# Work placed in the drain of the last attention layer of a fused conv/attention/MoE network

## The chip, the cores and the metric

The kernel runs on one core of a Trainium2 chip. The metric is the time of one execution on the device, in microseconds; lower is better. Three runs of the kernel before took 864.22, 866.94 and 872.31 us (median 866.94 us).

## The reference

The network has four layers on 16 images of 96 channels and 16 x 16 pixels (4096 tokens of 96 channels). Layers 0 and 1 are convolution-like token mixers, layer 2 is causal attention and a binarised feed-forward net, and layer 3 is causal attention and a mixture of four experts. What bears on this case is layer 3:

```python
t = t + _L3_attn_ref(_ln_t(t), ...)            # causal attention, 6 heads of 16, 256 tokens an image
t = t + _L3_ffn_ref(_ln_t(t), ...)             # the mixture of experts:
scores = jnp.einsum('bsd,de->bse', x, gate_w) + gate_b
probs = jax.nn.softmax(scores, axis=-1)
topk_vals, topk_idx = jax.lax.top_k(probs, 2)
mask = jnp.sum(jax.nn.one_hot(topk_idx, 4), axis=-2)
masked = probs * mask
masked = masked / (jnp.sum(masked, axis=-1, keepdims=True) + 1e-09)
h = jax.nn.gelu(jnp.einsum('bsd,edh->ebsh', x, w1) + b1[:, None, None, :], approximate=False)
y = jnp.einsum('ebsh,ehd->ebsd', h, w2) + b2[:, None, None, :]
out = jnp.einsum('bse,ebsd->bsd', masked, y)
```

## The kernel before, in words

Five engines run programs of their own and meet at semaphores. TensorE (PE) multiplies, VectorE (DVE) and ScalarE (ACT) empty PSUM, GpSimd (POOL) works on SBUF alone, SyncE (SP) issues the DMAs. The order on each engine is written out by hand; nothing is planned at run time. The tokens' residual stream is kept in `tok` (tokens on the partitions), the normed input of the next stage in `xn` (channels on the partitions, 4096 tokens wide), and the residual by channels in `xc`. PSUM is one tile `ps` of eight banks.

**Attention of layer 3.** A loop runs over the 16 images with three units of two heads each: scores (L890, and the mask at L894), maxima (DVE L1414), exponentials (ACT L549), transposes of the probabilities (PE L1071), copies of those to SBUF (ACT L536, DVE L1530), products with the values (PE L959). Scores and queries run two images ahead, so the loop also makes scores and stacked keys for two images that do not exist; SP stacks queries and keys by DMA into `qk` (L251), eight DMAs an image. The work behind an image's attention follows one image later: its outputs to SBUF (ACT L575), transposed (PE L930), normalised (DVE L1440, L1447), transposed back (PE L937), copied (ACT L580), projected (PE L951), added to `tok` (DVE L1454). Statistics of the finished tokens (DVE L1467, L1473), the inverse deviation (ACT L587, L589), the norm (POOL L344 to L349), a transpose (PE L944, `image_back`) and a copy (DVE L1459) put the image into `xn`.

**The drain.** After the loop nothing is left to overlap with. The outputs of image 15 go through the chain just named, and the norms of images 14 and 15 through theirs, one step after the other.

**The start of the mixture.** In the kernel before it follows the drain: PE transposes all of `tok` into channels in eight groups of four 128 x 96 tiles (L1197) and ACT copies each group into `xc` (L737). ACT splits the first two groups of 512 tokens of `xn` into a high part (`split_high`, L741), DVE makes the low part (L1671). PE makes the gate's logits, one 128-token tile of `xn` as weights and a moving operand of four columns, 32 tiles (L1202); a float32 product of this kind is two passes, so there are 64 records. DVE and ACT (L1676 to L1705) turn the logits into gate values; PE transposes these (L1238), DVE copies them to `gate_t` (L1729), and SP stores them and loads them back broadcast over the channels (L277, L274). PE has meanwhile made three steps of the experts' first product (`hidden`, L1217, three float32r matmuls each: high by high, high by low, low by high). From the fourth on it alternates `hidden(n)` and `expert_out(n - 3)` (L1228) for 96 steps in all. Each step's result passes two Gelus on ACT (L754, L757) and a subtraction on DVE (L1726) before `expert_out` reads it. DVE weights an expert's output by the gate (L1720), POOL adds it to `xc` (L464), and SP stores eight groups to the output.

Each engine waits in its own order. On DVE, `split`, the gate's chain, the first L1726, and then the copy to `gate_t` come in that order. The first Gelu needs a load of the activation table, which stands in ACT's program directly before it.

## Time and profile before

| | |
|---|---|
| median of 3 runs | 866.94 us |
| the profiled execution: time | 873.87 us |
| the profiled execution: span | 872.1 us |
| granted TensorE clock, mean | 0.935 |
| PE busy | 788.7 us (90%) |
| DVE busy | 592.1 us (68%) |
| ACT busy | 575.1 us (66%) |
| POOL busy | 263.3 us (30%) |

All places in time below are microseconds from the start of the span of the profiled execution. An engine's busy share is an average over stages with different limits; what counts for a change in one place is which wait ends last there. The granted clock is a share of TensorE's full speed: 1.00 is 2.4 GHz, 0.50 is 1.2 GHz, and a value between them is a stretch that holds some of both. "Idle before, releaser" in brackets is how long the engine had stood idle before the row and what let it go.

### The profile page before, as it was taken

Reading aid. Unit: us, or ns where it says so; the run is one execution under the profiler, and the core shown is the slowest. Engines: PE = TensorE matmul, PEld = TensorE weight load, DVE = VectorE, ACT = ScalarE, POOL = GpSimd, SP = SyncE. Lnnn points to the kernel's source line nnn. Section 1 sums busy time; section 2 is a strip of 40 time slices with the busy share of each in tenths; the row PEclk is TensorE's granted clock in tenths of the full one; section 3 lists DMA queues with packets and bytes.
Section 4 is the critical chain, followed back from the end, with each engine's and each line's share of the span. In section 5 each row is a group of like instructions: output and inputs, shape, how many; then the busy total and the mean of one; then the engine's idle time right before and its main releaser. Section 6 shows DMA issues by size and latency. Waiting matters only on the chain.

```text
span 872.1 us, 17805 instructions
## 1 busy us (share of the span) xinstructions
PE 788.7 (90%) x5497; PEld 602.9 (69%) x5497; DVE 592.1 (68%) x1537; ACT 575.1 (66%) x1403; POOL 263.3 (30%) x516
## 2 busy tenths in 40 slices
PE   2998999999997989999997963799999978999997
PEld 1965778777886957777774662477777767777775
DVE  6156867667774347888883996478787814778876
ACT  3235877777775448888884723378888834788875
POOL 2702365556544441212120001112121110333434
PEclk9998999999998679999997996799999965999999
DMA  6000000111011123333330000323232302221320
GB/s 201 1 1 1 1 14 16 19 20 15 14 20 24 32 66 95 88 98 84 96 86 23 1 1 0 104 79 104 77 103 79 103 5 55 60 53 45 79 59 19
DMA packets 63271, 44.48 MB, mean 51 GB/s; under 512 B 34416, under 2 KB 55280, under 8 KB 63088
## 3 DMA queue, kind: packets, MB, share of 16 engines
q1 hardware_dynamic: 63216, 43.78, 20.0%
q8 instruction: 30, 0.49, 0.3%
q14 instruction: 25, 0.20, 0.1%
HBM read 12.24 MB, written 3.21 MB: 18 GB/s over the span
## 4 chain that ended last, share of the span: by engine, by line
PE 76%; DVE 10%; issue 6%; ACT 3%; POOL 3%; DMA 2%; SPq 1%; POOLq 0%; DVEq 0%
PE ps L1071 12%; PE ps L959 9%; PE ps L883 9%; PE ps L1217 7%; PE ps L1228 7%; PE ps L890 5%; PE ps L894 4%; PE ps L907 3%; PE ps L908 2%; PE ps L921 2%; PE ps L930 2%; PE ps L951 2%; PE ps L833 2%; PE ps L1202 1%; POOL onn L387 1%
## 5 line engine op out<-in xcount | busy, mean ns | idle before, releaser
L549 ACT ACTIVATE ee<-ps,nmax 128x128 f32<-128x128 f32 (+1 forms) x584 | 207.4, 443 | 11.5 <-DVE nmax L1414 7.7
L1071 PE MATMUL ps<-w,ee 128*128 128x128 f32 x960 | 141.1, 275 | 3.2 <-ACT big L536 0.9
L1071 PEld LDWEIGHTS ps<-w,ee 128*128 128x128 f32 x960 | 111.6, 142 | 25.1 <-issue 9.9
L1414 DVE TENSOR_REDUCE nmax<-ps 128x2 f32<-128x256 f32 x200 | 101.8, 551 | 34.4 <-PE ps L894 33.6
L536 ACT ACTIVATE big<-ps 128x512 f32<-128x512 f32 (+1 forms) x192 | 97.1, 548 | 22.5 <-PE ps L1071 22.3
L1726 DVE TENSOR_TENSOR hhl<-ee,hhl 128x512 fp32r<-128x512 f32 x96 | 80.6, 845 | 31.5 <-ACT hhl L757 30.0
L883 PE MATMUL ps<-kh,big 128*128 128x256 f32 x384 | 94.5, 390 | 2.2 <-POOL big L327 1.2
L1411 DVE TENSOR_REDUCE nmax<-ps 128x4 f32<-128x1024 f32 x48 | 58.8, 1224 | 55.6 <-PE ps L883 55.6
L959 PE MATMUL ps<-big,vh 128*32 128x256 f32 (+1 forms) x1188 | 92.6, 354 | 0.0
L464 POOL TENSOR_TENSOR xc<-big,xc 96x512 f32<-96x512 f32 x32 | 52.4, 1638 | 111.4 <-DVE big L1720 111.2
L1217 PE MATMUL ps<-qk,w1hl 128*128 128x512 f32 x288 | 85.4, 407 | 0.4 <-DVE ee L1729 0.4
L883 PEld LDWEIGHTS ps<-kh,big 128*128 128x128 f32 x384 | 71.4, 193 | 18.0 <-ACT ee L549 6.4
L1228 PE MATMUL ps<-hhl,w2hl 128*96 128x512 f32 x288 | 83.1, 398 | 0.5 <-DVE hhl L1726 0.5
L327 POOL TENSOR_TENSOR big<-qs,w 96x256 f32<-96x256 f32 x90 | 52.0, 610 | 100.3 <-ACT qs L559 72.3
L754 ACT ACTIVATE ee<-ps 128x512 f32<-128x512 f32 x96 | 57.5, 599 | 30.2 <-PE ps L1217 30.2
L1530 DVE COPY big<-ps 128x384 f32<-128x384 f32 x96 | 52.8, 550 | 32.1 <-PE ps L1071 32.1
L344 POOL COPY onn<-tok 128x192 f32 (+1 forms) x31 | 10.7, 344 | 190.2 <-ACT lnr L589 190.2
L959 PEld LDWEIGHTS ps<-big,vh 128*32 128x32 f32 x1188 | 40.0, 110 | 40.2 <-issue 22.3
L1217 PEld LDWEIGHTS ps<-qk,w1hl 128*128 128x128 f32 x288 | 56.3, 196 | 16.1 <-DVE ee L1729 0.7
L1561 DVE BATCH_NORM_STATS2 est<-ee 128x6 f32<-128x256 f32 x192 | 66.9, 411 | 0.0
L1228 PEld LDWEIGHTS ps<-hhl,w2hl 128*96 128x96 f32 x288 | 47.1, 164 | 18.9 <-issue 1.0
L890 PE MATMUL ps<-qk 64*128 64x128 f32 (+1 forms) x400 | 50.8, 333 | 7.5 <-DMA qk<-hl 5.7
(257 smaller groups left out, 1369.4 us busy)
## 6 DMA issues: line engine op xcount, KB each, us to landing
qk<-hl SPq DMA_DIRECT2D x288, 96.0 KB, 3.1
big<-moe_gate SPq DMA_DIRECT2D x8, 768.0 KB, 6.9
w<-w_in SPq DMA_DIRECT2D x1, 1735.0 KB, 13.5
xc<-x_in SPq DMA_DIRECT2D x4, 384.0 KB, 6.5
l_mix<-on SPq DMA_DIRECT2D x32, 48.0 KB, 2.1
tok<-l_mix SPq DMA_DIRECT2D x16, 96.0 KB, 2.0
out<-xc SPq DMA_DIRECT2D x8, 192.0 KB, 2.1
w<-w_in SPq DMA_DIRECT2D x1, 998.0 KB, 9.9
```

The lines of the kernel that those rows point to most:

```text
L536: nc.scalar.activation(et[:, h, 0:w], ps[:, 4 + hh, 0:w], ACT.Copy).then_inc(own(l, f"et{hh}"), 1)
L549: last = nc.scalar.activation(ee[:, ke, hh, qc, 0:w], src, ACT.Exp, bias=nmax[:, kp, hh, qc:qc + 1])
L883: last = mm(ps[:, 2 * kp + hh, qc * N:(qc + 1) * N], qh[:, par, 2 * u + hh, qc * P:(qc + 1) * P], kh[:, par, :], start=True, stop=True)
L890: mm(ps[:, 2 * kp + hh, qc * N:qc * N + w], qk[r0:r0 + 4 * HD, par, u, 0, qc * P:(qc + 1) * P], qk[r0:r0 + 4 * HD, par, u, 1, 0:w], start= ...
L959: last = mm(ps[32 * r:32 * (r + 1), 6, g * N + q0:(g + 1) * N], vh[:, par, tc, 3 * g + r, :], et[:, 3 * g + r, tc * N:tc * N + N - q0], st ...
L1071: last = nc.tensor.transpose(ps[:, 4 + hh, b * P:(b + 1) * P], ee[:, u, hh, qc, tc * P:(tc + 1) * P], ident)
L1217: last = mm(ps[:, 4 + n % 4, :], w1hl[:, w, s * P:(s + 1) * P], xhl[:, t % 2, x, :], start=(k == 0), stop=(k == 2))
L1228: last = mm(ps[0:C, e, :], w2hl[:, w, s * C:(s + 1) * C], hhl[:, n % 4, h, :], start=(j == 0 and k == 0), stop=(j == NJ - 1 and k == 2))
L1411: last = V.tensor_reduce(out=nmax[:, kp, :, :].rearrange("p h q -> p (h q)"), in_=src, axis=AX.X, op=ALU.max, negate=True)
L1414: last = V.tensor_reduce(out=nmax[:, kp, :, qc], in_=ps[:, 2 * kp:2 * kp + 2, qc * N:qc * N + scores_cols(l, qc)], axis=AX.X, op=ALU.max, ...
L1561: last = V.bn_stats(est[:, par, q, 2 * u + hh, :], ee[:, u, hh, q, :])
L1726: V.tensor_tensor(hhl[:, n % 4, 1, :], hf[:, n % 4, :], hhl[:, n % 4, 0, :].bitcast(F32), ALU.subtract).then_inc(sg("moe_lo"), 1)
```

## The change

All of it is at the end of layer 3's attention and the start of the mixture.

- **Gate logits** (`gate_logits(tiles)`) go one tile at a time, each behind a wait for the image it reads, into bank 3 instead of bank 0 of PSUM. Tiles 0 and 1 come before the last image's `outputs`, tiles 2 and 3 before `outputs_back`, tile 4 after it, tiles 5 to 13 after the projection and the moved transposes, tiles 14 to 31 after the last `image_back`. In front of the first stand waits for the last maxima and exponentials, which use that bank.
- **Residual by channels**: groups 0 to 2 are transposed (PE, `residual_to_channels`) after the last projection, and copied (ACT, `residual_channels`) between the copy of `oc` and the last `deviation`. Groups 3 to 7 come after all logits on PE, and on ACT after the gate's exponential, ahead of the table load for Gelu. They use three banks in turn instead of four.
- **Splits** of the first two token groups move up on ACT to the place between image 14's `deviation` and the copy of `oc` (L580), behind waits for the last scores, for four finished images and for all DMAs that stack into `qk`, whose space they take; the low parts follow on DVE after `normalise_outputs` of image 15.
- PE's wait for all eight copied groups moves to the place before the transpose of the gate values. DVE waits for 32 logit increments instead of 8.

```diff
--- before.py
+++ after.py
@@ -569,6 +569,17 @@
                         act.wait_ge(*upto(l, f"stacked{par}", m * STK))
                     nc.scalar.activation(hl[:, par, :, 0, :], ps[0:C, 7, :].rearrange("p (a t) -> p a t", a=2), ACT.Copy).then_inc(own(l, "hi"), 1)
 
+            def residual_channels(g):
+
+                act.wait_ge(sg("xres_ps"), g + 1)
+                nc.scalar.activation(xc[:, g * 512:(g + 1) * 512], ps[0:C, g % 3, :], ACT.Copy).then_inc(sg("xres"), 1)
+
+            def split_high(t):
+
+                if t >= 2:
+                    act.wait_ge(sg("moe_h_ps"), NS * (t - 1))
+                nc.scalar.activation(xhl[:, t % 2, 0, :], xn[:, t * 512:(t + 1) * 512], ACT.Copy).then_inc(sg("moe_xhi"), 1)
+
             def outputs_to_sbuf(l, i):
 
                 act.wait_ge(*upto(l, "av", i + 2))
@@ -689,8 +700,18 @@
                 outputs_to_sbuf(l, B - 1)
                 if l > 1:
                     deviation(l, B - 2, 0)
+                if l == 3:
+                    act.wait_ge(*upto(3, "s_ps", 3 * B + 2))
+                    act.wait_ge(*upto(3, "xn", 4))
+                    for par in range(2):
+                        act.wait_ge(*upto(3, f"stacked{par}", STK * (B // 2 + 1)))
+                    split_high(0)
+                    split_high(1)
+                if l > 1:
                     outputs_by_channel(l, B - 1)
                 if l == 3:
+                    for g in range(3):
+                        residual_channels(g)
                     deviation(l, B - 1, 1)
                 if l == 1:
                     inverse_root(B)
@@ -732,21 +753,10 @@
                             act.wait_ge(sg("f2_quant"), g + 1)
                             nc.scalar.activation(y1[:, :, g * GT:(g + 1) * GT], y1[:, :, g * GT:(g + 1) * GT], ACT.Gelu,
                                                  scale=amax[:, 0, g:g + 1]).then_inc(sg("f2_gelu"), 1)
-            for g in range(8):
-                act.wait_ge(sg("xres_ps"), g + 1)
-                nc.scalar.activation(xc[:, g * 512:(g + 1) * 512], ps[0:C, g % 4, :], ACT.Copy).then_inc(sg("xres"), 1)
-            def split_high(t):
-                if t >= 2:
-                    act.wait_ge(sg("moe_h_ps"), NS * (t - 1))
-                nc.scalar.activation(xhl[:, t % 2, 0, :], xn[:, t * 512:(t + 1) * 512], ACT.Copy).then_inc(sg("moe_xhi"), 1)
-
-            act.wait_ge(*upto(3, "xn", B))
-            for par in range(2):
-                act.wait_ge(*upto(3, f"stacked{par}", STK * (B // 2 + 1)))
-            split_high(0)
-            split_high(1)
             act.wait_ge(sg("f3_gl"), 1)
             nc.scalar.activation(gate[:, 1, :, :], gate[:, 0, :, :], ACT.Exp).then_inc(sg("f3_gexp"), 1)
+            for g in range(3, 8):
+                residual_channels(g)
             for n in range(NS * NB):
                 act.wait_ge(sg("moe_h_ps"), n + 1)
                 if n >= 4:
@@ -999,6 +1009,20 @@
                     last = mm(y, xc[:, a:a + P], wb("ident", C)[:, 0:C], start=False, stop=True)
                 last.then_inc(sg("l1_y_ps"), 1)
 
+            def residual_to_channels(g):
+
+                if g >= 3:
+                    pe.wait_ge(sg("xres"), g - 2)
+                for t in range(4):
+                    last = nc.tensor.transpose(ps[0:C, g % 3, t * P:(t + 1) * P], tok[:, g * 4 + t, :], ident)
+                last.then_inc(sg("xres_ps"), 1)
+
+            def gate_logits(tiles):
+
+                for t in tiles:
+                    pe.wait_ge(*upto(3, "xn", t // TPI + 1))
+                    mm(ps[:, 3, t * NE:(t + 1) * NE], xn[:, t * P:(t + 1) * P], wa("f3_gate"), start=True, stop=True).then_inc(sg("f3_gl_ps"), 1)
+
             def normed_back(g):
 
                 pe.wait_ge(sg("l1_normed"), g + 1)
@@ -1111,6 +1135,10 @@
                 weigh_values(l, (B - 1) % 2, 1).then_inc(own(l, "av"), 1)
                 if l == 1:
                     output_sums(B - 2, B + 1)
+                if l == 3:
+                    pe.wait_ge(*upto(l, "max", 3 * B + 2))
+                    pe.wait_ge(*upto(l, "exp", 6 * B + 2))
+                    gate_logits(range(0, 2))
                 outputs(l, B - 1)
                 if l == 1:
                     pe.wait_ge(sg("l1_exp"), 6 * B)
@@ -1145,13 +1173,21 @@
                     score_unit(2, 0, 1, 1, 1)
                     pe.wait_ge(sg("l2_xn"), 8)
                 if l > 1:
+                    if l == 3:
+                        gate_logits(range(2, 4))
                     outputs_back(l, B - 1)
+                    if l == 3:
+                        gate_logits(range(4, 5))
                     pe.wait_ge(*upto(l, "v_sb", B + 1))
                     image_back(l, B - 2, 0)
                     project_outputs(l, B - 1)
                 if l == 3:
+                    for g in range(3):
+                        residual_to_channels(g)
+                    gate_logits(range(5, 14))
                     pe.wait_ge(*upto(l, "added", B + 1 + START))
                     image_back(l, B - 1, 1)
+                    gate_logits(range(14, NT))
 
                 if l > 1:
                     pe.wait_ge(*upto(l, "max", 3 * B + 2))
@@ -1190,22 +1226,8 @@
                                         last = mm(ps[:, 6 + b, t * C:(t + 1) * C], y1[:, j, a:a + P],
                                                   wb("f2_w2")[:, j * C:(j + 1) * C], start=(j == 0), stop=(j == NJ - 1))
                                 last.then_inc(sg("f2_y2_ps"), 1)
-            for g in range(8):
-                if g >= 4:
-                    pe.wait_ge(sg("xres"), g - 3)
-                for t in range(4):
-                    last = nc.tensor.transpose(ps[0:C, g % 4, t * P:(t + 1) * P], tok[:, g * 4 + t, :], ident)
-                last.then_inc(sg("xres_ps"), 1)
-
-            def gate_logits(g):
-                for t in range(4 * g, 4 * g + 4):
-                    last = mm(ps[:, 0, t * NE:(t + 1) * NE], xn[:, t * P:(t + 1) * P], wa("f3_gate"), start=True, stop=True)
-                last.then_inc(sg("f3_gl_ps"), 1)
-
-            pe.wait_ge(sg("xres"), 8)
-            pe.wait_ge(*upto(3, "xn", B))
-            for g in range(8):
-                gate_logits(g)
+            for g in range(3, 8):
+                residual_to_channels(g)
 
             def hidden(n):
                 t, s = n // NS, n % NS
@@ -1235,6 +1257,7 @@
             for n in range(LAG):
                 hidden(n)
             pe.wait_ge(sg("f3_gate"), 1)
+            pe.wait_ge(sg("xres"), 8)
             nc.tensor.transpose(ps[:, 0, P:2 * P], gate[:, 0, :, :].rearrange("p t e -> p (t e)"), ident).then_inc(sg("moe_gate_ps"), 1)
             pe.wait_ge(sg("moe_gate_t"), 1)
             for n in range(LAG, NS * NB):
@@ -1585,6 +1608,10 @@
                     dve.wait_ge(*upto(l, "bn", B - 1))
                     image_moments(l, B - 2, 0)
                 normalise_outputs(l, B - 1)
+                if l == 3:
+                    for t in range(2):
+                        dve.wait_ge(sg("moe_xhi"), t + 1)
+                        V.tensor_tensor(xhl[:, t, 1, :], xn[:, t * 512:(t + 1) * 512], xhl[:, t, 0, :].bitcast(F32), ALU.subtract).then_inc(sg("moe_x"), 1)
                 if l > 1:
                     dve.wait_ge(*upto(l, "out_ps", B + 1))
                     image_channels(l, B - 2)
@@ -1666,13 +1693,10 @@
                             link(V.scalar_tensor_tensor(out=tv, in0=v, scalar=-QB + QEPS, in1=tv, op0=ALU.max, op1=ALU.add))
                             link(token_stats(range(6 * g, 6 * g + 6 if g < NG - 1 else NT)))
             dve.wait_ge(*upto(3, "xn", B))
-            for t in range(2):
-                dve.wait_ge(sg("moe_xhi"), t + 1)
-                V.tensor_tensor(xhl[:, t, 1, :], xn[:, t * 512:(t + 1) * 512], xhl[:, t, 0, :].bitcast(F32), ALU.subtract).then_inc(sg("moe_x"), 1)
-            dve.wait_ge(sg("f3_gl_ps"), 8)
+            dve.wait_ge(sg("f3_gl_ps"), NT)
 
             gl, ge = gate[:, 0, :, :], gate[:, 1, :, :]
-            gp = ps[:, 0, 0:NT * NE].rearrange("p (t e) -> p t e", e=NE)
+            gp = ps[:, 3, 0:NT * NE].rearrange("p (t e) -> p t e", e=NE)
             link(V.tensor_reduce(out=st[:, 0, :], in_=gp, axis=AX.X, op=ALU.max))
             V.tensor_tensor(gl, gp, last_dim(st[:, 0, :], NE), ALU.subtract).then_inc(sg("f3_gl"), 1)
             dve.wait_ge(sg("f3_gexp"), 1)
```

## Rows read from the trace of the kernel before

**Rows 1.** Busy time by stretch (us, busy, records, then granted clock, DMA share, GB/s).
```profile
713.10:725.80 12.70, 12.69 (x65) 12.70 (x66) 1.29 (x2) 0.98 (x2) 0.00 (x0) 0.55 0.00 0
725.80:738.30 12.50, 10.16 (x23) 6.95 (x24) 8.09 (x33) 6.81 (x12) 0.00 (x0) 0.50 0.22 44
738.30:863.00 124.70, 124.70 (x541) 94.20 (x540) 97.30 (x125) 99.80 (x186) 48.20 (x29) 1.00 0.26 59
```

**Rows 2.** Busy time and granted clock of the microseconds in which the clock changes.
```profile
700.00:701.00 1.00, 0.59 (x3) 0.37 (x4) 0.03 (x1) 0.38 (x1) 0.61 (x2) 0.87 0.00 0
710.00:711.00 1.00, 1.00 (x7) 0.93 (x6) 0.00 (x0) 0.64 (x2) 0.00 (x0) 0.51 0.00 0
714.00:715.00 1.00, 1.00 (x9) 1.00 (x8) 0.99 (x2) 0.08 (x1) 0.00 (x0) 0.70 0.00 0
738.00:739.00 1.00, 1.00 (x5) 0.76 (x4) 0.69 (x1) 0.01 (x1) 0.00 (x0) 0.85 0.85 131
```

**Rows 3.** The drain, in order of time: start, us, what, idle before and releaser.
```profile
700.08 0.42 PE L937 MATMUL ps<-w,ob 128*96 128x128 f32 x2 [0.78 <-DVE ob L1447]
...
700.54 0.38 ACT L580 ACTIVATE oc<-ps 96x256 f32<-96x256 f32 x1 [1.43 <-PE ps L937]
...
701.26 1.01 PE L951 MATMUL ps<-w,oc 97*128 97x96 f32 x4
...
703.76 0.29 ACT L587 ACTIVATE lnr<-cmv,eps 128x2 f32<-128x2 f32 x1 [2.84 <-DVE cmv L1473]
...
706.01 0.63 PE L944 MATMUL ps<-w,onn 128*96 128x128 f32 x2 [3.74 <-POOL onn L349]
```

**Rows 4.** Residual transposes, their copies and the splits, in order of time.
```profile
706.44 5.89 PE L1197 MATMUL ps<-w,tok 128*96 128x128 f32 x32
...
707.53 0.59 ACT L737 ACTIVATE xc<-ps 96x512 f32<-96x512 f32 x1 [3.24 <-PE ps L1197]
708.39 0.59 ACT L737 ACTIVATE xc<-ps 96x512 f32<-96x512 f32 x1 [0.26 <-PE ps L1197]
...
712.93 1.15 ACT L741 ACTIVATE qk<-xn 128x512 fp32r<-128x512 f32 x2
```

**Rows 5.** One line each: four-column matmuls before 714.6, after 716, and L833.
```profile
L1202 PE MATMUL ps<-w,xn x13: 253/253/356, 713.1 to 714.5; 128*128 128x4 f32 x13
...
L1202 PE MATMUL ps<-w,xn x46: 354/354/354, 715.8 to 725.4; 128*128 128x4 f32 x46
...
L833 PE MATMUL ps<-stf,xn x64: 354/354/376, 20.1 to 33.6; 96*128 96x4 f32 x64
```

**Rows 6.** From the last logit to the steady part, in order of time.
```profile
725.63 4.19 PE L1217 MATMUL ps<-qk,w1hl 128*128 128x512 f32 x9
725.81 0.29 DVE L1676 TENSOR_REDUCE st<-ps 128x32 f32<-128x128 f32 x1 [10.82 <-PE ps L1202]
...
726.79 1.28 ACT L754 ACT_TABLE_LOAD   x1
...
728.58 0.59 ACT L757 ACTIVATE hhl<-ps 128x512 fp32r<-128x512 f32 x1
...
731.34 0.38 DVE L1705 TENSOR_TENSOR gate<-gate,st 128x128 f32<-128x128 f32 x1
...
731.56 0.68 DVE L1726 TENSOR_TENSOR hhl<-ee,hhl 128x512 fp32r<-128x512 f32 x1
...
732.28 0.29 DVE L1729 COPY ee<-ps 128x128 f32<-128x128 f32 x1
...
732.63 1.65 PE L1217 MATMUL ps<-qk,w1hl 128*128 128x512 f32 x3 [0.38 <-DVE ee L1729]
```

**Rows 7.** DMAs that stack into qk, last eight, and their landing (first and last start).
```profile
L251 SPq DMA_DIRECT2D qk<-hl x8: 583/599/612, 691.9 to 696.3; - x8
...
DMA to landing us min/median/max: 3.0/3.2/3.2
```

**Rows 8.** Landing of the first two gate loads, issued at 734.2 and 734.6.
```profile
DMA to landing us min/median/max: 6.8/8.1/9.5
```

## The prediction

> **What bounds the kernel now.** I read the page's chain of waits first. It is PE for three quarters, and in the attention of layer 3 PE has no gaps. So a gain can only come from a stretch where PE stands still or runs slowly. The busy time by stretch gives three [rows 1]: 12.7 us of gate logits at a mean clock of 0.55, 12.5 us from the last logit to the steady part of the mixture at 0.50, and 124.7 us of steady mixture with PE busy throughout at full clock. The last must be paid whatever happens before it, so the end moves exactly as much as its begin.
>
> The timeline of the drain comes next [rows 3]. Ahead of L937 PE stands for 0.78 us; there are three such holes between 698 and 701. The last `deviation` runs at 703.76 and PE gets the last image at 706.01, 2.25 us later, after a chain through ACT and POOL. Then work follows that needs hardly anything of the drain: 32 residual transposes from 706.44 [rows 4], and logits from 713.1 [rows 5]. DVE starts on the logits at 725.81, and PE's fourth `hidden` starts at 732.63, 6.82 us later, released by the copy to `gate_t` [rows 6].
>
> The clock [rows 2]: it falls during 700 (mean 0.87), in the thin drain; it rises at the very end of 710, when PE has done nothing but transposes for 4.5 us; it falls during 714 with the four-column matmuls, 1.4 us after the first, and rises only at 738.3 (mean 0.85), after 5.7 us of unbroken expert matmuls. PE counts as busy all through the logits, and they still hold the clock down.
>
> **Prices.** A pass of a logit at full clock: 13 starts from 713.1 to 714.5, 1.4/12 = 0.117 us. At half clock: 46 from 715.8 to 725.4, 9.6/45 = 0.213 us [rows 5]. The new code waits and increments for each tile. L833 is the same form with a wait for each tile, 64 passes from 20.1 to 33.6: 13.5/63 = 0.214 us. So the wait costs nothing at half clock. The increment of each tile isn't shown; its nearest row is a whole hand-over, copy included, from L1729 at 732.28 to PE at 732.63 [rows 6], 0.35 us. I take zero, as L833's price lies on the pass alone, and keep 0.35 us a tile as the upper end. Below zero it can't go, as the passes stay.
> A group of four residual transposes takes 708.39 - 707.53 = 0.86 us at half clock; its copy starts 707.53 - 706.44 = 1.09 us after its first transpose and takes 0.59 us [rows 4].
>
> **The drain, step by step.** Logits 0 to 3 are 4 passes before L930 and 4 before L937, 0.47 us each time at full clock, in holes of the kind of 0.78 us. Tile 4 is 2 passes, 0.23 us, in the third. Cost nothing.
> Splits on ACT: they wait for the last stacking DMA, started at 696.3 and landing 3.2 us later, 699.5 [rows 7]. Two splits take 1.15 us [rows 4], so ACT is free at about 700.7, where the copy of `oc` began at 700.54 and ended at 700.92; PE read it at 701.26 [rows 3]. The 0.2 us go into that slack of 0.34 us: nothing. Were the DMA later, each us would be one in the whole chain. The low parts on DVE end by 702, before L951 ends at 702.27; behind them only the wait for L951 is queued. Where they stood before, they lay beside the logits, so their leaving saves nothing either.
> Three residual groups on PE: from 702.1, as the first transpose starts 0.2 us before its forerunner's end [rows 3, 4], to 702.1 + 3 x 0.86 = 704.7. ACT copies them at 703.2, 704.05 and 704.9, and ends at 705.5. **The last `deviation` is queued behind**, and POOL, PE and DVE wait for it: 705.6 instead of 703.76, so image 15 is ready for PE at 706.01 + 1.8 = 707.8. This is the price of the move.
> PE fills that time with tiles 5 to 13, 18 passes: to 704.7 + 2.1 = 706.8 at full clock or + 3.8 = 708.5 at half. By its own history the clock should be back around 704 or 705, after transposes as dense as those before 710.98. I take 708.0 for L944.
> Then 36 passes stand open: 0.43 us to the first (706.44 - 706.01), 35 x 0.213 = 7.5, and 0.4 from the last start to DVE: **logits done at 716.3 instead of 725.81, 9.5 us earlier**. Bounds: 716.9 at half clock throughout (8.9); 707.8 + 0.4 + 35 x 0.117 + 0.4 = 712.7 at full (13.1). I stay near the half-clock end, since 1.4 us of these matmuls were followed by the fall.
>
> **From logits to steady part.** ACT is free 0.98 us after DVE's start (726.79 - 725.81), where the table load stood [rows 6]. Now five residual copies come first, paced by PE: the last starts at 0.98 + 4 x 0.86 = 4.4 and ends at 5.0. From the table load's start to the end of the first L757 there are 729.17 - 726.79 = 2.4 us, so 7.4; then the first L1726 at 7.5 in place of 5.75; from there 1.07 us to the fourth `hidden`: 8.55 instead of 6.82, **1.7 us lost**. Before, DVE's gate chain was last there (L1705 ends 5.9 us after the start); now ACT is. Lower bound 0.6: copies paced by their own 0.59 us end at 0.98 + 2.95 = 3.9, which puts the first L1726 at 6.4. Upper bound 2.4: at half clock PE needs 4.3 + 4.2 us for 20 transposes and 9 `hidden` matmuls, then 0.9 for the gate's transpose and copy.
> The fourth `hidden` is then at 716.3 + 8.55 = 724.85, 7.8 us earlier.
> **The clock after it.** Before, 732.63 to 738.30 ran at half: 5.67 us, 2.8 us lost. Now 20 transposes and 9 `hidden` matmuls stand ahead of it without a logit, 8 us of what raised the clock before. Full clock from the start gives 2.8 back. Against it: PE idles 1 to 2 us before the fourth `hidden`, and a relapse as long as the full stretch from 711.0 to 714.4 costs 1.7, leaving 1.1. I take 2.3.
> A second look at that place: the gate loads land 6.8 us after issue [rows 8], some 8.4 us after the fourth `hidden`, and DVE comes to them at n = 6, at full clock after about 7 us. It waits 1.5 us; PE needs its next low part 10.4 us in, DVE has it at about 10.0. Nothing, by a narrow margin.
>
> **Sum.** 9.5 - 1.7 + 2.3 = 10.1 us, against the profiled execution's 873.87 (span 872.1): 863.8. That execution is 6.9 us above the median of the runs; taken from the median 866.94, the same 10.1 us give 857.
>
> **The rivals.**
> *The clock stays at half* through drain, logits and hand-over. For it: it fell during 700 in a drain that stays thin, and logits never raised it. Against: the 12 transposes now in the drain. Gain 8.9 - 2.4 + 1.1 = 7.6: 859.3.
> *Transposes don't bring the clock back* at all, in the drain or in the hand-over, and it returns only after the expert matmuls, as before: 8.9 - 2.4 + 0 = 6.5 us: 860.4. Against it stands the row of the rise: nothing but transposes for 4.5 us before it [rows 2, 4].
> The Trainium skill, "TensorE: Matmul & The Clock Gate", Part 4, says that the full clock does not engage for transpose-mode work, which doesn't count as PE-busy in the same way. It would make this rival the forecast; the trace disagrees with it at 710.98.
> *The clock is full over the logits too.* 13.1 - 0.6 + 2.3 = 14.8: 852.1. Between this and the forecast lies every mixture.
> *Moved logits are dearer.* 0.35 us more for each of the 18 open tiles: 6.3 us less, 3.8 us gained: 863.1.
> *The change does not do what it says*: 18 of 32 tiles and five of eight groups still stand open after the drain; if the drain filled up as much as it took over, only the 14 tiles' 28 passes would count, 6 us, less 1.7: 862.6.
> *Slower.* The gate loads land late. Place: DVE, after n = 6, with PE's next `expert_out` behind it. Up to a landing of about 7.2 us it is free, past that each us is a us. To be slower than before it must eat 10 us, a landing of 17 us; 20 us would give 869.8. The two loads seen took 6.8 and 9.5 [rows 8], and only the first is waited for.
>
> **Chances.** Forecast 0.50 (gain 8.5 to 12, 855 to 858.5), half clock 0.17, no clock from transposes 0.06, fuller clock 0.10, dearer logits 0.07, drain filled 0.05, slower 0.05. One per cent is 8.7 us, about what a measurement of this kernel tells from no change; the three runs before lie 8 us apart. The forecast passes it with 0.44 of its 0.50, the fuller clock with all; half clock with 0.06. Faster 0.60, same 0.35, slower 0.05. The range takes in all but the slow case and the far end of the fuller clock: 851 to 864, with some room above for the scatter of the runs.
>
> **What would show it.** In the profile after: logit records between 698 and 709; the second `deviation` near 705.6; L1676 near 716; ACT's table load about 5 us after it; the fourth `hidden` near 725 and a granted clock near 1.00 within 4 us of it; PE without gaps after. I am wrong if L951 starts later than 701.5 (splits on the path), if L1676 comes after 718, or if PE waits inside the steady part.

## The result, and the profile after

Over 19 runs each, taken side by side, the changed kernel takes 858.18 us (855.04 to 865.73) and the kernel before 866.87 us (862.88 to 874.54). The ratio is 0.990, interval 0.987 to 0.993: 8.7 us between the medians, where 10.1 us and 857 us were forecast. The gain in the medians is one per cent, and the interval leaves out 1. In a later session, 12 runs of the changed kernel beside 17 of the one before gave the ratio 0.990 again (0.987 to 0.993).

The profiled execution of the changed kernel took 855.99 us with a span of 854.1 us: 18.0 us less span than that of the kernel before, twice what the medians say. The chain of waits shows where the surplus lies (start, us, what; the last product with the values in layer 3). Before it stood at 696.54, and after:

```profile
690.90 1.55 PE ps L969 x24
...
696.27 2.57 PE ps L1017 x12
```

So 5.6 us of the 18 arise ahead of the drain, where the two programs are the same. For the rest of this text **the drain begins** at the end of that product, 698.06 in the profile before and 692.43 after, 0.04 us before ACT's copy of `ots`, and all distances count from there. From the drain's begin to the end of the span it is 174.0 us before and 161.7 us after: 12.3 us less.

The timeline after answers to [rows 3, 4]. Start, us, what, and in brackets the idle time before with its releaser:

```profile
692.35 0.61 PE L1024 MATMUL ps<-w,xn 128*128 128x4 f32 x4
...
693.50 0.53 PE L1024 MATMUL ps<-w,xn 128*128 128x4 f32 x4
...
693.98 1.15 ACT L581 ACTIVATE qk<-xn 128x512 fp32r<-128x512 f32 x2 [0.50 <-DMA qk<-hl]
...
694.45 0.42 PE L947 MATMUL ps<-w,ob 128*96 128x128 f32 x2 [0.41 <-DVE ob L1470]
...
694.71 0.28 PE L1024 MATMUL ps<-w,xn 128*128 128x4 f32 x2
695.04 0.36 ACT L591 ACTIVATE oc<-ps 96x256 f32<-96x256 f32 x1
...
695.45 0.82 PE L961 MATMUL ps<-w,oc 97*128 97x96 f32 x4
...
696.06 2.77 PE L1017 MATMUL ps<-w,tok 128*96 128x128 f32 x12
...
697.16 0.59 ACT L575 ACTIVATE xc<-ps 96x512 f32<-96x512 f32 x1 [1.76 <-PE ps L1017]
...
698.01 0.59 ACT L575 ACTIVATE xc<-ps 96x512 f32<-96x512 f32 x1 [0.26 <-PE ps L1017]
...
698.62 2.39 PE L1024 MATMUL ps<-w,xn 128*128 128x4 f32 x18
698.87 0.59 ACT L575 ACTIVATE xc<-ps 96x512 f32<-96x512 f32 x1 [0.26 <-PE ps L1017]
699.36 0.28 ACT L598 ACTIVATE lnr<-cmv,eps 128x2 f32<-128x2 f32 x1
...
701.60 0.40 PE L954 MATMUL ps<-w,onn 128*96 128x128 f32 x2 [0.59 <-POOL onn L349]
...
701.83 6.89 PE L1024 MATMUL ps<-w,xn 128*128 128x4 f32 x36
```

The reader is to see three things. The first ten passes of the logits (a pass is one of the two records of a tile) lie in the holes, and the chain around them goes on as before: the projection L961 starts 3.0 us into the drain (before 3.2). The last `deviation` (L598) has lost its place: it starts when ACT has made its third residual copy, 6.9 us in instead of 5.7, and the last image reaches PE at 9.2 instead of 7.9. And the 36 passes that stay open take 6.9 us.

The hand-over, answering to [rows 6]:

```profile
708.87 0.29 DVE L1700 TENSOR_REDUCE st<-ps 128x32 f32<-128x128 f32 x1 [6.42 <-PE ps L1024]
...
712.72 2.45 PE L1239 MATMUL ps<-qk,w1hl 128*128 128x512 f32 x9
...
713.71 1.28 ACT L764 ACT_TABLE_LOAD   x1
...
714.39 0.39 DVE L1729 TENSOR_TENSOR gate<-gate,st 128x128 f32<-128x128 f32 x1
...
715.50 0.59 ACT L767 ACTIVATE hhl<-ps 128x512 fp32r<-128x512 f32 x1
...
716.20 0.69 DVE L1750 TENSOR_TENSOR hhl<-ee,hhl 128x512 fp32r<-128x512 f32 x1 [1.41 <-ACT hhl L767]
...
717.14 0.96 PE L1239 MATMUL ps<-qk,w1hl 128*128 128x512 f32 x3 [1.87 <-DVE ee L1753]
```

DVE has its gate values at 714.8 and then stands idle for 1.41 us until ACT, late through its five copies and the table load, has made the first Gelus. The fourth `hidden` starts 8.27 us after the logits are done, which here and below means DVE's start on them; before it was 6.82.

The granted clock after, in the microseconds in which it changes (the number before the last two), answering to [rows 2]:

```profile
695.00:696.00 1.00, 0.80 (x6) 0.72 (x7) 1.00 (x2) 0.40 (x2) 0.06 (x1) 0.93 0.00 0
699.00:700.00 1.00, 1.00 (x10) 1.00 (x9) 0.00 (x0) 0.85 (x3) 0.06 (x1) 0.86 0.00 0
702.00:703.00 1.00, 1.00 (x10) 1.00 (x10) 0.42 (x1) 0.00 (x0) 0.00 (x0) 0.85 0.00 0
712.00:713.00 1.00, 1.00 (x6) 0.96 (x5) 0.93 (x9) 0.59 (x1) 0.00 (x0) 0.53 0.00 0
```

It falls 3.4 us into the drain, is full again from 6.9, falls with the logits at 10.3, and is full from 20.5, four us before the fourth `hidden`, until the last two us of the span. Before, it was full without a break only from 40.2, nearly six us after the fourth `hidden`.

### The profile page after: what moved, and what is told of

The parts are those of the page before. It is cut to its first block, busy times and chain, and to the rows that moved or that the text cites. A ratio compares the mean times of both kernels' runs of the same rounds, so it can differ in the third digit from the quotient of the medians.

```text
span 854.1 us, 17807 instructions
## 1 busy us (share of the span) xinstructions
PE 778.4 (91%) x5497; PEld 595.6 (70%) x5497; DVE 592.4 (69%) x1537; ACT 575.2 (67%) x1403; POOL 264.5 (31%) x516
## 4 chain that ended last, share of the span: by engine, by line
PE 76%; DVE 9%; issue 6%; ACT 3%; POOL 3%; DMA 2%; SPq 1%; POOLq 0%; DVEq 0%
PE ps L1095 12%; PE ps L969 9%; PE ps L893 9%; PE ps L1239 7%; PE ps L1250 7%; PE ps L900 5%; PE ps L904 4%; PE ps L917 3%; PE ps L918 2%; PE ps L931 2%; PE ps L961 2%; PE ps L940 2%; PE ps L843 2%; POOL onn L387 1%; DVE amax L1669 1%
## 5 line engine op out<-in xcount | busy, mean ns | idle before, releaser
L1239 PE MATMUL ps<-qk,w1hl 128*128 128x512 f32 x288 | 82.1, 394 | 1.9 <-DVE ee L1753 1.9
L1239 PEld LDWEIGHTS ps<-qk,w1hl 128*128 128x128 f32 x288 | 54.0, 188 | 16.9 <-DVE ee L1753 2.2
## 6 DMA issues: line engine op xcount, KB each, us to landing
w<-w_in SPq DMA_DIRECT2D x1, 1735.0 KB, 12.7
```

The costliest lines, as they stand in the source:

```text
L1239: last = mm(ps[:, 4 + n % 4, :], w1hl[:, w, s * P:(s + 1) * P], xhl[:, t % 2, x, :], start=(k == 0), stop=(k == 2))
```

## The experiments

Each is read from its own profile in the same distances, since those see tenths of a microsecond where the times of a few runs scatter by nine. "Logits done" is DVE's start on them, and "drain to end" runs from the drain's begin to the end of the span. The last column is the ratio of the times to those of the kernel before in the same session, with its interval and the number of runs. The intervals of all these kernels but the last one overlap that of the change: what a single edit is worth is shown by the profiles, one or two for each kernel, and not by the times.

| | last `deviation` | last `image_back` | logits done | fourth `hidden` after that | drain to end | ratio of the times |
|---|---|---|---|---|---|---|
| before | 5.7 | 7.9 | 27.7 | 6.8 | 174.0 |  |
| before, second profile | 5.1 | 7.3 | 24.2 | 6.7 | 169.3 |  |
| the change | 6.9 | 9.2 | 16.4 | 8.3 | 161.7 | 0.990 (0.987 to 0.993), 19 |
| the change, second profile | 7.0 | 9.2 | 16.6 | 8.1 | 161.7 | 0.990 (0.987 to 0.993), 12 |
| logits late | 7.0 | 9.3 | 22.7 | 8.3 | 167.8 | 0.994 (0.990 to 0.998), 10 |
| residual groups late | 5.4 | 7.7 | 15.9 | 9.9 | 164.3 | 0.991 (0.988 to 0.995), 10 |
| splits late | 6.7 | 8.9 | 15.8 | 8.4 | 161.1 | 0.991 (0.988 to 0.995), 10 |
| deviation first | 5.2 | 8.4 | 15.0 | 8.3 | 160.7 | 0.988 (0.981 to 0.995), 4 |
| Gelu table early | 7.1 | 9.3 | 17.3 | 6.9 | 161.1 | 0.986 (0.978 to 0.995), 4 |
| wide logits | 5.6 | 7.9 | 12.4 | 6.8 | 158.3 | 0.985 (0.976 to 0.995), 4 |
| transposes in the holes | 5.2 | 7.5 | 15.7 | 8.3 | 160.9 | 0.986 (0.977 to 0.994), 4 |
| three together | 5.2 | 7.5 | 12.0 | 6.9 | 155.8 | 0.982 (0.974 to 0.991), 4 |
| three together, second profile | 5.2 | 7.5 | 12.0 | 6.9 | 156.4 | 0.982 (0.977 to 0.986), 6 |

**Logits late.** The change with all 32 tiles behind the last `image_back`:

```diff
-                    gate_logits(range(0, 2))
...
-                        gate_logits(range(2, 4))
...
-                        gate_logits(range(4, 5))
...
-                    gate_logits(range(5, 14))
                     pe.wait_ge(*upto(l, "added", B + 1 + START))
                     image_back(l, B - 1, 1)
-                    gate_logits(range(14, NT))
+                    gate_logits(range(0, NT))
```

> The changed kernel with all 32 gate-logit tiles back behind the last image_back; residual groups and splits stay moved. Counted from the end of the last product with the values (start of the drain), the changed kernel has the logits done 16.4 us in and the fourth hidden 24.7 us in. My theory (28 of the 64 passes are hidden in waits of the drain): image_back does not move (9.2 us in, set by ACT's copies before deviation), then 64 passes at half clock, 13.6 us: logits done near 23.5, about 7 us later, and the kernel about 7 us slower than the changed one. Rival (the clock is what was gained, the logits' place is worth little): the passes run at full clock for the most part, 7.5 us, logits done near 17.5, 1 us slower.

`image_back` stays where it is and the logits are done 6.2 us later, 28 passes at 0.22 us. The drain to the end is 6.1 us longer; the median is 863.67 us over 10 runs. The passes run at half clock for the most part (64 of them take 13.0 us), so the rival is out: half of the 12.3 us between the first pair of profiles is these 28 passes in waits.

**Residual groups late.** Groups 0 to 2 back to the other five:

```diff
 # ACT
-                    for g in range(3):
-                        residual_channels(g)
                     deviation(l, B - 1, 1)
...
-            for g in range(3, 8):
+            for g in range(8):
                 residual_channels(g)
 # PE
-                    for g in range(3):
-                        residual_to_channels(g)
                     gate_logits(range(5, 14))
...
-            for g in range(3, 8):
+            for g in range(8):
                 residual_to_channels(g)
```

> The changed kernel with residual groups 0 to 2 moved back to the other five, behind the logits on PE and behind the gate's exponential on ACT. My theory: deviation goes back to 5.7 us into the drain and image_back to about 7.9, but PE has no transposes to raise its clock, so the logits run at half: done at 16.2 to 16.6, no gain; then eight copies before the table load instead of five, the fourth hidden 10.9 us after the logits instead of 8.3: 2 to 3 us slower than the changed kernel. Rival (the three copies ahead of deviation cost more than they give): logits done 1.8 us earlier and the same end or faster.

`deviation` goes back to 5.4, but the logits are done only 0.5 us earlier than in the change: without the twelve transposes the clock, fallen at 3.4, isn't full again before 20.5. The hand-over grows to 9.9 us, one less than I expected, and the clock relapses once more after it, at 27.3, which costs 1.4 us. In all 2.6 us longer: the direction is my theory's, and that the size is too is in part luck, since the relapse made up for a hand-over I had put too long.

**Splits late.** Both halves of the split back where they were, ACT's ahead of its wait for the logits:

```diff
-                    split_high(0)
-                    split_high(1)
                 if l > 1:
                     outputs_by_channel(l, B - 1)
...
+            split_high(0)
+            split_high(1)
             act.wait_ge(sg("f3_gl"), 1)
```

> The changed kernel with the two splits back where ACT waits for the logits (and their low parts on DVE there). My theory: they cost nothing in either place: no difference above 0.3 us in the drain's length to the logits' end. Rival (the wait for the stacking DMA and 1.15 us of splits sit ahead of the copy of oc, on the path): logits done 0.3 to 1.2 us earlier.

The rival had the better of this one. Everything is 0.25 us earlier from `deviation` on, and the logits' end 0.6 us. The row above shows the place: in the change ACT waits 0.50 us for the stacking DMA, its splits end at 695.1, and the copy of `oc` starts at 695.04, 0.17 us behind the end of L947; here it follows at 0.04 us:

```profile
695.91 0.42 PE L946 MATMUL ps<-w,ob 128*96 128x128 f32 x2 [0.41 <-DVE ob L1469]
...
696.37 0.38 ACT L591 ACTIVATE oc<-ps 96x256 f32<-96x256 f32 x1 [1.43 <-PE ps L946]
```

The move of the splits is a small loss, 0.6 us from the drain to the end by either profile of the change. The three parts of the change, each taken back alone, are worth 6.1, 2.6 and -0.6 us, 8.1 together.

**Deviation first.** ACT's last `deviation` ahead of the three copies:

```diff
+                    deviation(l, B - 1, 1)
                     for g in range(3):
                         residual_channels(g)
-                    deviation(l, B - 1, 1)
```

> The changed kernel with ACT's last deviation ahead of the three residual copies. My theory (the copies delay image 15 by some 1.2 us in the trace, 6.9 instead of 5.7 us into the drain, but PE is busy with logits 5 to 13 until 8.6 us in): image_back at 8.6 instead of 9.2, logits done 0.5 us earlier. If the copies' delay was the whole price (rival): 1.2 to 1.8 us earlier.

The logits are done 1.5 us earlier, three times what I expected and within what the rival said. But the copies' delay is not the whole price: `deviation` runs 1.7 us earlier, and PE reaches `image_back` only 0.75 us earlier, since it is indeed busy with tiles 5 to 13, without a wait before L954. The other 0.7 us is clock: the fall comes at 10.3 us in either kernel, and the open passes have that much more of the full stretch ahead of it.

```profile
702.67 0.30 ACT L598 ACTIVATE lnr<-cmv,eps 128x2 f32<-128x2 f32 x1 [2.29 <-DVE cmv L1496]
...
703.53 2.47 PE L1024 MATMUL ps<-w,xn 128*128 128x4 f32 x18
...
705.86 0.40 PE L954 MATMUL ps<-w,onn 128*96 128x128 f32 x2
```

**Gelu table early.** The table load directly behind the gate's exponential:

```diff
             nc.scalar.activation(gate[:, 1, :, :], gate[:, 0, :, :], ACT.Exp).then_inc(sg("f3_gexp"), 1)
+            nc.scalar.preload_act_table_set("gelu_and_others")
             for g in range(3, 8):
                 residual_channels(g)
```

> The changed kernel with the table load for Gelu put directly behind the gate's exponential, ahead of the five residual copies on ACT. In the changed kernel the load starts 4.84 us after the logits' end and the fourth hidden 8.27 us after it. My theory (ACT's late load is last in the hand-over): load near 1.0, copies done near 5.0, first Gelu near 5.0 instead of 6.1, DVE's gate chain ends at 5.9 and becomes last, fourth hidden near 7.1, 1.1 to 1.2 us earlier. Rival (PE's 20 transposes and nine hidden matmuls are last): fourth hidden unchanged at 8.2 or more.

```profile
710.65 0.29 DVE L1701 TENSOR_REDUCE st<-ps 128x32 f32<-128x128 f32 x1 [7.13 <-PE ps L1025]
...
711.63 1.28 ACT L758 ACT_TABLE_LOAD   x1
...
717.57 0.96 PE L1240 MATMUL ps<-qk,w1hl 128*128 128x512 f32 x3 [0.62 <-DVE ee L1754]
```

From the logits to the fourth `hidden` it is 6.9 us instead of 8.3: ACT's late table load was last, and now DVE's gate chain is. Of these 1.35 us only 0.6 reach the end of this profile, because the clock fell 0.6 us earlier in this drain and the logits were done 0.9 us later.

**Wide logits.** The moving operand of each logit takes 128 columns instead of four; the surplus is overwritten by the next tile or never read:

```diff
-mm(ps[:, 3, t * NE:(t + 1) * NE], xn[:, t * P:(t + 1) * P], wa("f3_gate"), start=True, stop=True)
+mm(ps[:, 3, t * NE:t * NE + P], xn[:, t * P:(t + 1) * P], w96[:, C96["f3_gate"][0]:C96["f3_gate"][0] + P], start=True, stop=True)
```

> The changed kernel with the moving operand of each gate-logit matmul 128 columns wide instead of 4 (the gate's four columns and the 124 weight columns beside them); a later tile overwrites the surplus of an earlier one. Pass by pass the weight load of 128 columns is the same, and transposes with 128 moving columns take 0.109 and 0.214 us, as the narrow logits do with 0.117 and 0.213. My theory (it is the four columns that let the clock fall, not the waiting): the clock, up at 6.8 us into the drain, stays up through the logits; 36 passes take about 4.0 us instead of 6.7, logits done near 13.7 instead of 16.4, the transposes behind them at full clock, fourth hidden about 20.8 us in instead of 24.7: 3 to 4 us faster. Rival (the clock follows PE's idle time in the drain, whatever a matmul's width): no change of clock, and no gain or a small loss.

```profile
698.14 0.29 ACT L598 ACTIVATE lnr<-cmv,eps 128x2 f32<-128x2 f32 x1
...
700.39 0.39 PE L954 MATMUL ps<-w,onn 128*96 128x128 f32 x2 [0.85 <-POOL onn L349]
...
700.62 4.18 PE L1024 MATMUL ps<-w,xn 128*128 128x128 f32 x36
...
704.96 0.29 DVE L1700 TENSOR_REDUCE st<-ps 128x32 f32<-128x128 f32 x1 [3.71 <-PE ps L1024]
```

The 36 open passes take 4.2 us instead of 6.9 for 32 times the columns. The clock does not fall in the drain at all:

```profile
695.00:696.00 1.00, 0.90 (x8) 0.65 (x8) 1.00 (x2) 0.48 (x2) 0.16 (x1) 1.00 0.00 0
700.00:701.00 1.00, 0.61 (x6) 0.64 (x7) 0.17 (x1) 0.00 (x0) 0.25 (x1) 1.00 0.00 0
...
713.00:714.00 1.00, 1.00 (x4) 0.76 (x3) 0.51 (x2) 0.87 (x2) 0.00 (x0) 0.55 0.00 0
716.00:717.00 1.00, 1.00 (x5) 0.79 (x4) 0.69 (x1) 0.03 (x1) 0.00 (x0) 0.75 0.91 141
```

Even the ten passes in the holes, now wide, hold it up where it fell before. The logits are done 12.4 us in, four us earlier than in the change; I had expected 13.7, without the clock's gain on the transposes, and so on `deviation`, before them. The fourth `hidden` starts 5.5 us earlier (19.2 for 24.7), as the faster transposes also bring ACT's copies and its table load forward. But 2.1 us of it are lost again: the clock relapses from 713 to 716, beginning 1.3 us after the fourth `hidden`. No run shows why it does here and in two other profiles, and not in the rest. Drain to end is 3.4 us shorter than in the change.

**Transposes in the holes.** Residual groups 0 to 2 where tiles 0 to 4 were, and those behind the projection:

```diff
-                    gate_logits(range(0, 2))
+                    residual_to_channels(0)
                 outputs(l, B - 1)
...
-                        gate_logits(range(2, 4))
+                        residual_to_channels(1)
                     outputs_back(l, B - 1)
...
-                        gate_logits(range(4, 5))
+                        residual_to_channels(2)
...
-                    for g in range(3):
-                        residual_to_channels(g)
+                    gate_logits(range(0, 5))
                     gate_logits(range(5, 14))
```

> The changed kernel with residual groups 0, 1 and 2 transposed in the three holes of PE in the first 3 us of the drain, and gate tiles 0 to 4 where they were, behind the last projection. My theory (transposes count for the clock, narrow logits do not): the fall of the clock at 3.4 us into the drain does not come, the projection ends some 0.4 us earlier, deviation is back near 5.3; later the logits let it fall all the same, so logits done 0.5 to 1.5 us earlier than 16.4. Rival (the clock falls because PE waits, whatever fills the holes): it falls at 3.4 as before, and there are fewer transposes later to raise it: logits done later than 16.4.

```profile
699.00:700.00 1.00, 1.00 (x11) 1.00 (x11) 1.00 (x3) 1.00 (x3) 0.00 (x0) 1.00 0.00 0
700.00:702.00 2.00, 2.00 (x20) 2.00 (x20) 0.83 (x5) 0.65 (x3) 0.39 (x2) 1.00 0.03 8
702.00:703.00 1.00, 0.69 (x5) 0.60 (x4) 0.00 (x0) 0.00 (x0) 0.92 (x2) 0.56 0.00 0
```

The drain begins at 695.7 here, and the fall at 3.4 us does not come; after 28 narrow passes the clock falls at 6.4, and the 36 open ones all run at half. The logits are done 0.7 us earlier. So twelve transposes hold the clock in the three holes in which ten narrow passes did not. With narrow passes or nothing there, the first fall came 2.7 to 3.8 us into the drain in all nine such profiles, wherever the drain began.

**Three together.** Deviation first, Gelu table early and wide logits in one kernel.

> The changed kernel with deviation ahead of the residual copies, the Gelu table load ahead of the five copies, and 128-column gate logits. If the three are independent: logits done near 12.5 us into the drain, fourth hidden near 19.3 instead of 24.7, and the kernel about 5 us faster than the changed one, near 853 to 854. If the hand-over has another floor (DVE's gate chain, 6.8 us from logits to fourth hidden), it cannot go below that: 12.5 + 6.8.

The clock is at 1.00 from the drain's begin to the last 2 to 3 us of the span, in both profiles, the logits are done at 12.0, and DVE's gate chain sets the 6.9 us after them. Drain to end is 5.9 us shorter than in the change, 5.3 us in the second profile.

**The kernel before, the change and the three together, once more.**

> The kernel before, unchanged, for a second profile. My theory (the scatter of some 9 us between executions arises ahead of the changed part, where the program is the same, through the phase of the clock's changes): the drain begins anywhere between 692 and 702 us, and from there to the end of the span it takes 171 to 174.5 us. Rival (the scatter lies in the part that was changed): the drain begins near 698, and what follows differs by several us from 174.

> The changed kernel, unchanged, for a second profile and more times. My theory: from the drain's begin to the end of the span 161 to 163.5 us, wherever the drain begins; median of the runs 857 to 861, some 9 to 12 us below the kernel before. Rival (the 12 us of the first pair of profiles were luck of the clock's phase in the drain): 164 us or more.

> The three edits together once more (deviation first, Gelu table early, 128-column logits), beside the changed kernel on the same chip. From the drain's begin to the end of the span 155.5 to 157 us, with no fall of the clock in the drain; median about 5 us below the changed kernel's, ratio to the kernel before 0.98 to 0.985.

The drains begin at 694.7 (before), 700.7 (change) and 692.1 us (three together), and over all profiles between 692.1 and 701.1: up to nine us of scatter that no edit here touches. It goes with the clock: where the granted clock is at half around 76 us, as in the first line (before) and not in the second (the change), the drain begins late. Busy time and granted clock from 76 to 83 us:

```profile
76.00:83.00 7.00, 6.14 (x23) 3.57 (x24) 2.67 (x8) 1.87 (x6) 0.32 (x1) 0.51 0.01 2
...
76.00:83.00 7.00, 6.82 (x44) 5.29 (x45) 3.01 (x8) 5.50 (x15) 0.27 (x1) 1.00 0.00 0
```

Five profiles of both kernels and their variants have a mean of 0.51 to 0.53 in this stretch and a drain that begins at 697.4 or later; two have 0.76 and begin at 695.6 and 695.7; six have 1.00 and begin between 692.1 and 694.7. What makes the clock fall there in some executions stays open.

The change repeats its 161.7 us to the tenth. The kernel before does not: 169.3 after 174.0, below the 171 I had set. In its second profile some of the 64 open passes find the full clock, and they take 10.5 us where they took 12.7 before; the last two lines are the clock ahead of them and 3.5 us into them:

```profile
702.51 5.05 PE L1197 MATMUL ps<-w,tok 128*96 128x128 f32 x32
...
708.44 10.45 PE L1202 MATMUL ps<-w,xn 128*128 128x4 f32 x64 [0.88 <-ACT xc L737]
...
718.92 0.29 DVE L1676 TENSOR_REDUCE st<-ps 128x32 f32<-128x128 f32 x1 [8.61 <-PE ps L1202]
...
708.00:709.00 1.00, 0.56 (x5) 0.56 (x6) 0.00 (x0) 1.00 (x3) 0.00 (x0) 1.00 0.00 0
...
712.00:713.00 1.00, 1.00 (x8) 1.00 (x7) 0.00 (x0) 0.00 (x0) 0.00 (x0) 0.59 0.00 0
```

In times: three together 851.48 us (6 runs), the change 862.08 us (12 runs), before 869.42 us (17 runs), all on one chip; ratios to before 0.982 (0.977 to 0.986) and 0.990 (0.987 to 0.993). The intervals do not touch, if only just: the kernel with the three edits beats both. Two of the medians are not where I had them: the change is 7.3 us below the kernel before, not 9 to 12, and the three together are 10.6 us below the change, not 5. The profiles' drains account for 5.3 to 5.9 of these 10.6; six and twelve runs that scatter by eight and nine us can make up the rest, but no run shows that they do.

## Why the prediction was right

The time (858.18 us for 857) and the way were right. By the steps of the sum, against the first pair of profiles:

| step | forecast | measured |
|---|---|---|
| logits done earlier | 9.5 (8.9 to 13.1) | 11.3 |
| lost in the hand-over | 1.7 (0.6 to 2.4) | 1.45 |
| clock regained after the fourth `hidden` | 2.3 | 2.5 |
| sum | 10.1 | 12.3 |

- **What lies in holes costs nothing**: right for the logits; the projection came no later. The price of a pass with a wait and an increment of its own, which I had to bound at 0.35 us a tile, is zero: with the residual groups late the 36 open passes run at half clock throughout, with a wait and an increment for each tile, and start 0.209 us apart, for the 0.213 I took from the kernel before. The rival of dearer logits falls with it, and the late logits show that what was taken into the drain did not merely fill it up.
- **The splits cost nothing**: nearly. The slack of 0.34 us that I counted on at the projection was not there: it had come from PE being busy with `image_back`, and the copy of `oc` was delayed by 0.13 us. The late splits price the move at 0.6 us, some of it clock: the projection starts 3.0 us in with either, but its last pass falls behind the fall of the clock at 3.4 in the change, and not with the splits late.
- **The last `deviation` queued behind three copies**: the mechanism was right, the size less so, 1.2 us instead of 1.8. Of the 0.6, 0.4 is the projection, which I left where the profile before had it, and part of which now ran at full clock; the rest is that L598 starts ahead of the third copy's end. Against the run with `deviation` first, whose clock falls at the same place, the queue alone costs 1.7 us, which is the 1.8 of the sum.
- **The clock after the transposes**: right. I expected it back "around 704 or 705", 6 to 7 us into the drain, and it came at 6.9. The residual groups left late show the counterpart: without the twelve transposes it stays down until 20.5. The rival in which transposes don't bring the clock back is out, and so is the one of a clock at half throughout. The Trainium skill, "TensorE: Matmul & The Clock Gate", Part 4, says that the full clock does not engage for transpose-mode work. These rows, and those of the transposes in the holes, disagree with it.
- **The open passes**: put too long. I took them at half clock throughout, 7.5 us from the first to the last start, with `image_back` at 708.0, 9.9 us in. It came at 9.2, 0.8 us of the surplus in the first step; and from there the clock was full for 1.1 us more, which is where most of the other 1.0 us lies.
- **ACT is last in the hand-over**: right in mechanism and size (8.55 us expected, 8.27 measured), and the early table load takes it away.
- **The gate loads**, the one way to slower: DVE waits 2.02 us for the first one at n = 6, where I had 1.5, and PE runs on behind it. In the whole steady part PE waits once, 0.53 us for DVE at 848.4, where the profile before has no wait; the prediction's sign of being wrong was any wait there, and this one is too small to bear on the sum. The wait at n = 6 and PE beside it:

```profile
726.19 0.75 DVE L1744 SCALAR_TENSOR_TENSOR big<-ps,w,big 96x512 f32<-96x512 f32 x1 [2.02 <-DMA big<-moe_gate]
726.26 0.85 PE L1250 MATMUL ps<-hhl,w2hl 128*96 128x512 f32 x3
```

From the fourth `hidden` to the end it is 136.8 to 137.0 us in seven of the eleven profiles of changed kernels, 137.4 and 137.5 in two more, and 138.4 and 139.0 in the two with a relapse of the clock.

What the prediction lacked is how far the kernel before itself swings. The 12.3 us of the first pair and the 7.6 of the second (169.3 - 161.7) are both true, and that their mean, 10.0, is the forecast is luck as much as the sum. In the second pair the first step gives 7.6 us instead of 11.3, outside my bounds of 8.9 to 13.1, the hand-over costs 1.5 and the clock gives 1.5. The difference lies in the kernel before: its clock is full from 10.6 to 17.4 us into the drain in the second profile, over the end of the transposes and the first of the logits, and from 12.9 to 16.3 in the first. I took the reference from a single execution. So the hit of the median, 1.2 us off the forecast, says less for the sum than it seems.

What stays open: why the clock falls ahead of the drain in some executions and not in others. Some four us of the scatter are there at the end of layer 1 already: the last product with the values there starts at 270.3 and 265.9 in the two profiles of the kernel before, at 266.5 and 270.1 in those of the change.

## What to carry to other kernels

Before moving work into a drain, read what each engine has queued behind the place, and put the step on the critical chain first: three copies ahead of one small `deviation` cost 1.5 us at the logits' end, and a table load behind five copies another 1.35 in the hand-over. Ask of work that fills holes not only how long it takes but whether it holds TensorE's clock: here float32 matmuls whose weights change each time came 0.107 us apart with four moving columns and 0.112 us with 128, so the wider operand was nearly free, and it kept the clock up. And take the reference for a part from more than one profile, counted from a point that both kernels share.

## What the runs showed of the hardware that was not expected

- A float32 matmul with a fresh 128-column weight and a moving operand of 4 columns has nearly the same pitch as one with 128, at full clock 0.107 us for the first (18 passes with the Gelu table early) and 0.112 us for the second (36 passes of the wide logits).
- PE counted as fully busy with four-column matmuls never brought the clock from 1.2 to 2.4 GHz, and let it fall (64 passes before, 36 after, 28 with the transposes in the holes). Twelve transposes behind the projection brought it back, twelve in the holes kept it, and so did ten 128-column passes in the holes.
- Two profiles of the change reach the drain at 692.4 and 700.7 us, 8.3 us apart with the same instructions. The later one has 0.51 as its mean granted clock from 76 to 83 us, the earlier one 1.00.
